# Two-layer kernel (state-space scan, then routed FFN) on one core: Gelu straight from PSUM as soon as the last decay is made, and shorter first lists for the last round

## What is computed

```
attn:  xc, z = split(x @ W_in.T);  xs = silu(conv3(xc))
       dt = softplus(low-rank(xs)) + 1e-5;  Bp, Cp from xs
       A = exp(-exp(A_log) * dt)          # 16 states per channel
       s_t = A_t * s_{t-1} + Bp * dt * xs;  y = (Cp @ W_C.T) * s.sum(-1) + D * xs
       out = (y @ W_out.T) * silu(z)
ffn:   top 2 of 8 experts per token;  each: gelu(x @ W1[e] + b1) @ W2[e] + b2
       out = weighted sum of the two + gelu(x @ sW1 + sb1) @ sW2 + sb2
```

## Time and profile before

| what | value |
|---|---|
| median of 3 executions | 1243.47 us (1240.49 to 1244.02) |
| the profiled execution, its own time | 1239.15 us |
| its span, first to last instruction | 1237.3 us |
| PE busy | 1020.2 us (82%), 4704 matmuls |
| VectorE, ScalarE, GpSimd busy | 685.7, 620.3, 703.1 us |
| mean granted clock of TensorE | 0.903 |

### The profile page before, as it was taken

The page is one execution under the profiler, slowest core; times in us unless marked ns, Lnnn a source line. Parts: engine busy times, 40 slices in busy tenths (PEclk is TensorE's granted clock), DMA queues, the critical chain, the costliest instruction groups (busy, mean ns, idle before and its releaser), DMA issues.

```text
span 1237.3 us, 15570 instructions
## 1 busy us (share of the span) xinstructions
PE 1020.2 (82%) x4704; PEld 828.6 (67%) x4704; DVE 685.7 (55%) x1214; ACT 620.3 (50%) x1182; POOL 703.1 (57%) x700
## 2 busy tenths in 40 slices
PE   3445587877776878878789789999999999999996
PEld 2122265655554656656567578889899999998885
DVE  1699999999987988975986423111111111111233
ACT  3785869788485784595554332222222222232332
POOL 2496977868479896698677427533343333322211
PEclk9675789897877997897998989999999999999998
DMA  6000110202002016140533648398999998874511
GB/s 202 17 27 8 34 35 18 68 1 86 1 18 68 1 52 205 35 115 27 138 96 130 197 156 219 75 292 228 341 355 340 282 278 269 252 218 89 166 69 51
DMA packets 141779, 162.73 MB, mean 132 GB/s; under 512 B 28760, under 2 KB 126832, under 8 KB 141680
## 3 DMA queue, kind: packets, MB, share of 16 engines
q1 hardware_dynamic: 125824, 142.76, 35.7%
q0 software_dynamic: 15872, 18.99, 8.3%
HBM read 135.27 MB, written 26.87 MB: 131 GB/s over the span
## 4 chain that ended last, share of the span: by engine, by line
PE 52%; issue 13%; DVE 12%; POOL 12%; ACT 6%; SPq 3%; DMA 1%; DVEq 0%; POOLq 0%; ACTq 0%
PE psum L1013 22%; PE psum L980 11%; PE psum L969 6%; POOL Ssum L1533 6%; PE psum L992 6%; DVE S L1150 5%; DVE psum L1127 2%; PE psum L935 2%; ACT A L1415 1%; POOL list_d L1552 1%; PE psum L956 1%; DVE stats L1089 1%; POOL scale L1482 1%; ACT hT L1460 1%; DMA bb<-b 1%
## 5 line engine op out<-in xcount | busy, mean ns | idle before, releaser
L1533 POOL TENSOR_TENSOR Ssum<-Ssum,S 128x512 f32<-128x512 f32 x240 | 302.8, 1279 | 74.7 <-DVE S L1150 73.8
L1013 PE MATMUL psum<-w,hT 128*128 128x256 f32 x1152 | 264.1, 389 | 8.0 <-issue 6.0
L1583 POOL DMA_INDIRECT acc_d<-y,ID x72 | 114.2, 1586 | 248.3 <-DMA acc_d<-y,ID 119.9
L1013 PEld LDWEIGHTS psum<-w,hT 128*128 128x128 f32 x1152 | 223.0, 196 | 41.2 <-issue 8.0
L1415 ACT ACTIVATE A<-dts,nea 128x512 f32<-128x512 f32 x256 | 176.1, 718 | 85.9 <-DVE S L1150 62.6
L1454 ACT ACTIVATE hT<-psum,bb 128x256 f32<-128x256 f32 x200 | 83.6, 470 | 219.9 <-PE psum L980 219.8
L980 PE MATMUL psum<-XT,w 128*128 128x256 f32 x800 | 184.3, 388 | 11.5 <-issue 9.0
L1127 DVE TENSOR_TENSOR psum<-us,psum 128x512 f32<-128x512 f32 x256 | 163.5, 685 | 39.1 <-PE psum L901 37.6
L980 PEld LDWEIGHTS psum<-XT,w 128*128 128x128 f32 x800 | 154.1, 194 | 38.7 <-issue 14.3
L1150 DVE TENSOR_TENSOR_SCAN S<-A,carry,psum 128x512 f32<-128x512 f32 x120 | 148.9, 1269 | 0.0
L1284 DVE TENSOR_TENSOR y<-bb,psum 128x256 f32<-128x256 f32 x72 | 27.0, 416 | 212.2 <-PE psum L1013 212.1
(11 more groups left out here) (146 smaller groups left out, 1288.2 us busy)
## 6 DMA issues: line engine op xcount, KB each, us to landing
w<-W SPq DMA_DIRECT2D x94, 1024.0 KB, 7.5
bb<-b SPq DMA_DIRECT2D x47, 128.0 KB, 9.1
xnb<-x SPq DMA_DIRECT2D x16, 256.0 KB, 3.0
Xr<-x SPq DMA_DIRECT2D x16, 256.0 KB, 4.8
x_d<-gb SPq DMA_DIRECT2D x8, 512.0 KB
xn_d<-nb SPq DMA_DIRECT2D x8, 512.0 KB, 3.5
X<-x_d SPq DMA_DIRECT2D x16, 256.0 KB, 7.5
ACC<-acc_d SPq DMA_DIRECT2D x16, 256.0 KB, 5.7
```

What stands on the lines that cost most here:

```text
L1013: t = eng.matmul(bank(g)[:, 256 * k:256 * k + 256], hT[n % 2][:, f, 128 * k:128 * k + 128], w[:, f, :], start=f == 0, stop=f == 7)
L1533: eng.tensor_tensor(to, to, of, ALU.add).then_inc(nsum, 1)
L1583: eng.indirect_dma_start(acc_d, bass.IndirectOffsetOnAxis(ap=ID[:, col, 1:2].bitcast(u32), axis=0), y[n % NY][:, k, :], None, compute_op=A ...
```

## The change

```diff
 SETS = [ROUTED[a:b] for a, b in zip([0] + TILES, TILES[:-1])]
-SETS += [ROUTED[a:a + SET] for a in range(TILES[-2], len(ROUTED), SET)]
+SETS += [[group] for group in ROUTED[TILES[-2]:TILES[-2] + SET]]
+SETS += [ROUTED[a:a + SET] for a in range(TILES[-2] + SET, len(ROUTED), SET)]
...
     def route(r):
         while ROUND_END[r] - 1 not in posted:
             yield
-        yield
+        if not past[0]:
+            yield
         say("top2", r)
...
             say("ids", n)
-            for _ in range(4):
+            for _ in range(4 if len(SETS[n]) > 1 else 2):
                 yield
             listed[0] += len(SETS[n])
...
-        if direct:
+        if direct and past[0]:
             say("down_out", n, g)
         else:
             later(3, "down_out", n, g)
...
-    beside = pairs()
+    beside = itertools.chain(pairs(), direct())
...
                 part(beside, calls * (k + 1) // 32 - calls * k // 32)
+
+            ended[0] = decayed[0] == 32 * NC
         part(behind, 99)
         part(ahead, 99)
     last = post(NC - 1)
-    ended[0] = True
-    for _ in beside:
-        tick()
-        part(last, 1)
     past[0] = True
     say("widen")
     room_for[0] = NALL
-    beside = direct()
     for n, _ in enumerate(last):
         tick()
         part(beside, 1 + n % 2)
```

## The result

The changed kernel takes 1244.88 us (median of 15 executions, 1242.87 to 1247.47) against 1241.39 us of the kernel before on the same chip (15 executions, 1237.07 to 1244.02): ratio 1.0035, 95% interval 1.0023 to 1.0046. That is 3.5 us slower by the medians and 4.3 us by the ratio.

The account below looks back on a forecast made before the run. PE was taken as full from 880 us, with a list chain its work exactly covers before that. Weight delays of 2.8 to 4.3 us gave 3.5 us slower: 1243.47 + 3.5 = 1247.0 us, range 1237 to 1254.

Parts of the forecast that it names:

- it cancels: Rival: the idle time only moves from 715 to 800, 0 +- 2 us, 1243.5 us; chance 0.10.
- hole ahead of turn 13: PE finishes its remaining ups and downs at 798.4, then is idle for 12.6 us before up 23.
- slow clock behind it: After PE's idle time before up 23 the clock is at half for a while, costing 1.6 us.
- the 27 steps: Last post: 27 up and down steps on PE ahead of the logits instead of 12 or so, 46.6 us.
- the holes of 0.9 and 2.8: PE waits ahead of the logits: 0.9 us at turn 7, and one like the 2.82 at turn 8.
- the two scatters between the tables: Scatters 19 and 20 on GpSimd's queue among the 24 tables add 7.7 us, till 797.5.
- the 3.6 us that short lists save: The last round's first gather waits for one ids transfer instead of four, saving 3.6 us.
- what ends the hole: Rows land in 2.8 us, so up 23 could start at 809.6; w1 13 takes 6.3, giving 811.
- w1 26: Weight for up 24's second half, needed at 824.5, lands 9.2 us after issue: 2.8 us late in all.
- w2 28: Last awaited weight, for which PE waited at 875.10: 4.3 us later than before.
- the freed PE time wins: Rival: a shorter list chain starts up 23 near 806, 6 us faster, 1237.5 us; chance 0.27.
- SyncE's queue decides: Rival: later ids delay w2 28 at 875.10 by 14.6 us at most; 9 us slower, 1252.5 us; chance 0.23.

Follow-up runs that it names:

- e5: The changed kernel unaltered, run again on another chip: 1249.17 us, ratio 0.9999 to the kernel before.
- e3: The changed kernel with one call of direct at each step of the last post instead of one and two in turn: 1231.53 us, ratio 0.9872 to the kernel before.
- e8: The changed kernel with two calls of direct at each step of the last post: 1270.74 us, ratio 1.0165 to the kernel before.
- e9: The changed kernel with no call and one call of direct in turn at the last post's steps: 1236.93 us, ratio 0.9909 to the kernel before.
- e1: The kernel before with only the two list edits, a list each for the last round's first three groups: 1249.34 us, ratio 1.0000.
- e10: The changed kernel with one call per step and the last round's first three groups' weights fetched once experts are selected: 1230.95 us, ratio 0.9858 to the kernel before.
- e2: The changed kernel with the last round's lists in threes again, 4 calls apart: 1257.00 us, ratio 1.0066 to the kernel before.
- e7: The changed kernel with one call per step and the last round's lists in threes: 1235.81 us, ratio 0.9896 to the kernel before.
- e4: The changed kernel with the last round's first three groups' weights fetched once experts are selected, ahead of the lists: 1251.19 us, ratio 1.0020 to the kernel before.

## Why the prediction was right

Forecast +3.5 us with 1247.0 us; measured +3.5 by the medians (1244.88 us), +4.3 by the ratio, +4.1 by the profile. The 2.1 us between the two absolute figures are the base, whose median fell from 1243.47 to 1241.39 with 12 more executions. That the medians agree to the tenth is luck, and on another chip the change cost nothing (e5), which is the outcome of the rival "it cancels". By its steps, times less the 1.2 us:

| step | predicted | measured |
|---|---|---|
| hole of the last pair's Gelu goes | 8.40 to 0 | 8.40 to 0 |
| logits | 742.7 | 743.4 |
| first table | 759.3 | 760.8 |
| first ids | 801.0 | 802.0 |
| first gather issues | 804.2 | 805.1 |
| hole ahead of turn 13 | 12.6 | 12.8 |
| up 23 starts | 811.0 | 813.9 |
| slow clock behind it | 1.6 | 1.75 |
| up 24 starts | 820.9 | 824.0 |
| second half of down 26, against 875.10 | +2.8 to +4.3 | +4.4 |

- **The plan and the chain** held: the 27 steps, the holes of 0.9 and 2.8 (0.83 and 2.23), the two scatters between the tables, the 3.6 us that short lists save. e3, e8 and e9 show the mechanism itself: the logits move with the number of steps ahead of them. Counted from turn 6 they come after 30.1, 42.5, 61.9 and 78.1 us for 9, 18, 27 and 36 steps; nine steps are 15.6 us, and what differs from that is mostly holes of PE ahead of the logits, which each plan has in another number.
- **Mis-sized: what ends the hole.** I had the rows land in 2.8 us, from the gather of the earlier trace rows, and w1 13 in 6.3, the later of the two. It was the other way round. The chain of waits of the changed kernel has

```profile
807.57 5.49 DMA G<-xn_d,ID
813.19 1.09 PE psum L955 x4
```

 The second gather issued 0.4 us behind w1 13 and took 5.5 us. w1 13 landed in 4.9 us, in time. Up 23 came 2.9 us later than predicted.
- **Mis-sized: w1 26.** I gave up 24's second half 1.4 us of waiting; its 7.59 us against 7.31 leave 0.3. The weight was not faster: it issued at 816.74 and took 11.2 us to land instead of 9.2. PE came for it 3 us later than predicted. The two terms don't cancel: behind up 24 PE is 4.8 us late (turn 15 at 832.62 against 826.65, less 1.2), where 2.8 were predicted. That did not reach the end, since the next term decides there.
- **w2 28** issued at 870.79, that is 869.6, as worked out (869.5), and PE waited 1.05 us for it. It is the last wait, and it fixed the end at +4.4, the upper of my two bounds. The agreement is in part luck. The ids began 1.0 us later than predicted, and I counted one fetch less ahead of w2 28, where both plans have 14 behind the first ids. The seven ids less are right. What made up for both is that the issues of b1 and b2 held the queue for less: 11.8 us in all ahead of w2 28 instead of 17.1, summed over SyncE's timeline.
- **Rival "the freed PE time wins"** fell here because the chain was not shorter than my walk: up 23 came at 813.9, not near 806, though w1 13 did land in 4.9 us. Its premise was sound: e3 has 16 us of gain from the same idle time. What I had not priced is that one number of the change, the 1.5 calls a step, decides between it and my forecast.
- **Rival "SyncE's queue decides"**: its condition (w2 28 issued behind 869.5) was met by 0.1 us, and w2 28 did fix the end; what fell is its size, 4.4 us late at that place instead of 9 to 14.6. e1 and e10 speak against the queue as the bound of the time; e2 and e7 show it as the second in line, 2.5 to 8 us where w1 stands behind nine ids.
- That no Gelu goes straight from PSUM within the scan is shown by the plan of the changed kernel: `direct` begins at tick 255, and its first `up_out` comes behind the last `main` step. ScalarE's last decay starts at 658.1 and its load of the Gelu table at 675.8. The title's first half is true only of the last `post`.

## What to carry to other kernels

When independent work is woven into a serial chain on one in-order engine, the weaving ratio is a parameter of its own: count the engine's steps ahead of the chain's last link and the steps that are left as cover behind it, and choose the ratio where neither side runs dry. Removing a stall early in such a stretch (8.40 us here) only moves the idle time if the chain behind it is what the engine will wait for next. Measure the ratio's neighbours before judging the edit: here the same change is 0.3% slower or the same at 1.5 calls a step, 1.3 to 1.5% faster at 1 and 1.7% slower at 2.

## What the runs showed of the hardware that I had not expected

- A gather took longer to land the closer a 1 MB weight was issued ahead of it: 2.8 us with none, 4.5 us in e4 (weight 2.1 us ahead), 5.5 us in the changed kernel (0.4 us ahead). These are three single transfers.
- The kernel before took 1241.39 us on the first chip and 1248.4 to 1249.2 us on three others. Nine of the ten profiles made on those have the stretch described above, mostly from 770 to 792 us, in which matmuls come with gaps of 0.2 to 1.7 us, and in e5 ScalarE stands for 13.60 us. Its cause is open, and the kernel before was not profiled on those chips. It matters for the verdict: a kernel with a hole behind such a stretch loses less to it (3.3 of 8.6 us in e5), which fits the changed kernel's 1.0035 on one chip and 0.9999 on the other; that this is the reason is argued, not shown.
- After the hole of 12.81 us, 32 matmuls took 8.82 us instead of 7.07: part of them ran at 1.2 GHz (granted clock 0.50 from 806 to 816 and 1.00 again from 819).
